# Four-tile products in layers 1 and 2 of a compressed interaction network, and a part boundary at tile 12

## The reference

```
z  = relu(einsum('bhd,bkd,hks->bsd', x0, xk, W) + b)      # layers 0, 1, 2
xk = z[:, :64],  direct += z[:, 64:]                      # after layers 0 and 1
direct += z                                               # after layer 2
logit = sum over d of direct                              # 64 + 64 + 128 = 256 numbers a row
y = relu(relu([logit, dense] @ W1 + b1) @ W2 + b2) @ W3
```

## Time and profile before

| | us |
|---|---|
| median of 3 runs (lowest, highest) | 666.9 (666.8, 668.03) |
| the profiled execution | 669.69 |
| its span, first to last instruction | 667.9 |
| PE busy | 625.5 (94%) |
| DVE busy | 577.0 (86%), 507 instructions |
| POOL busy | 463.2 (69%) |
| ACT busy | 283.8 (42%) |
| mean granted TensorE clock | 0.995 |

### The profile page before, as it was taken

How to read it: one execution, slowest core, us unless ns; L and a number is a source line. 1 busy time by engine, 2 the same in 40 slices (tenths; PEclk the granted TensorE clock), 3 DMA queues, 4 the chain that set the end, 5 groups by cost and what they waited for, 6 DMA issues and landing times.

```text
span 667.9 us, 7153 instructions
## 1 busy us (share of the span) xinstructions
PE 625.5 (94%) x1916; PEld 358.0 (54%) x1916; DVE 577.0 (86%) x507; ACT 283.8 (42%) x341; POOL 463.2 (69%) x277
## 2 busy tenths in 40 slices
PE   0367999999999999999999999999999999999998
PEld 0124555565555555565655555555656555555553
DVE  4138899999999999999999999999999999999670
ACT  3004443544454444534454444444444544445323
POOL 6507768686887878786977878786878878716340
PEclk9997999999999999999999999999999999999999
DMA  6879586694939486785939495875939395862000
GB/s 226 186 189 222 118 202 133 149 199 93 217 84 227 94 195 139 174 174 117 221 80 216 82 218 114 189 159 135 212 93 216 77 225 105 199 131 67 0 1 0
DMA packets 27902, 98.19 MB, mean 147 GB/s; under 512 B 7473, under 2 KB 16433, under 8 KB 19826
## 3 DMA queue, kind: packets, MB, share of 16 engines
q1 hardware_dynamic: 20137, 90.92, 61.1%
q10 hardware_dynamic: 2633, 5.82, 3.0%
q0 software_dynamic: 5120, 1.32, 1.9%
HBM read 94.20 MB, written 3.84 MB: 147 GB/s over the span
## 4 chain that ended last, share of the span: by engine, by line
PE 85%; DVE 5%; DMA 3%; POOL 3%; issue 2%; ACT 1%; ACTq 0%; DVEq 0%; SPq 0%; POOLq 0%
PE z L527 40%; PE z L538 13%; PE z L533 12%; PE z L535 11%; PE z L518 4%; DVE products L405 4%; DMA x_rep<-x_rows 2%; PE z L521 2%; POOL gathered L361 1%; POOL low L309 1%; PE z L520 1%; PE spare L571 1%; PE z L595 1%; DVE low L309 1%; PE xk L595 1%
## 5 line engine op out<-in xcount | busy, mean ns | idle before, releaser
L405 DVE TENSOR_TENSOR products<-x_rep,xk 128x1024 f32<-128x1024 f32 (+1 forms) x288 | 366.7, 1333 | 28.1 <-ACT xk L621 27.2
L309 POOL TENSOR_TENSOR low<-products,high 128x1024 fp32r<-128x1024 f32 x112 | 265.0, 2391 | 134.2 <-ACT high L637 92.9
L527 PE MATMUL z<-products,w_whole 128*128 128x512 f32 x672 | 313.4, 599 | 0.0
L637 ACT ACTIVATE high<-products 128x1024 fp32r<-128x1024 f32 x176 | 184.3, 1056 | 243.0 <-DVE products L405 200.6
L361 POOL DMA_INDIRECT gathered<-in_tables,rows_sb x160 | 197.5, 1235 | 46.5 <-issue 44.2
L533 PE MATMUL z<-high,w_high 128*128 128x512 f32 x352 | 188.2, 535 | 16.5 <-ACT high L637 16.5
L527 PEld LDWEIGHTS z<-products,w_whole 128*128 128x128 f32 x672 | 128.6, 191 | 113.1 <-issue 98.3
L535 PE MATMUL z<-high,w_low 128*128 128x512 f32 x352 | 139.6, 397 | 0.0
L538 PE MATMUL z<-low,w_high 128*128 128x512 f32 x352 | 114.0, 405 | 4.3 <-DVE low L309 3.6
L533 PEld LDWEIGHTS z<-high,w_high 128*128 128x128 f32 x352 | 66.9, 190 | 62.3 <-issue 33.2
L309 DVE TENSOR_TENSOR low<-products,high 128x1024 fp32r<-128x1024 f32 x64 | 93.8, 1467 | 1.3 <-ACT high L637 1.3
(11 more groups left out here) (34 smaller groups left out, 102.8 us busy)
## 6 DMA issues: line engine op xcount, KB each, us to landing
x_rep<-x_rows SPq DMA_DIRECT2D x60, 768.0 KB, 16.4
x_rep<-x_rows SPq DMA_DIRECT2D x61, 512.0 KB, 9.3
x_rows<-gathered SPq DMA_DIRECT2D x15, 225.0 KB
x_rep<-in_w ACTq DMA_DIRECT2D x2, 1280.0 KB, 9.4
gathered<-in_tables,rows_sb POOLq DMA_INDIRECT x160
x_rep<-x_rows SPq DMA_DIRECT2D x4, 384.0 KB, 12.6
x_rep<-x_rows ACTq DMA_DIRECT2D x4, 384.0 KB, 19.0
x_same<-x_rows SPq DMA_DIRECT2D x15, 90.0 KB
```

The source lines that it names most:

```text
L309: ops.tensor_tensor(low[0:p, slot, 0:n, :], products[0:p, index % RING, 0:n, :], high[0:p, slot, 0:n, :].bitcast(fp32), ALU.subtract).then ...
L405: nc.vector.tensor_tensor(slots, rep, row.unsqueeze(1).broadcast_to([p, n, N]), ALU.mult).then_inc(made, 1 + pair)
L527: mm = nc.tensor.matmul(out, w_whole[0:p, at, i, :], products[0:p, slot, i, :], start=(t + i == 0), stop=(t + i == tiles[layer] - 1))
L637: nc.scalar.activation(high[0:p, slot, 0:n, :], products[0:p, index % RING, 0:n, :], ACT.Copy).then_inc(rounded, 1)
```

## The change

DVE makes four tiles in one instruction for eight pairs of groups rather than two: 0+1, 2+3, 4+5 and 6+7 in layer 1, and 14+15, 16+17, 18+19 and 20+21 in layer 2. Groups 6+7 hold tiles 12 to 15, and 20+21 likewise, so a part of the replicated inputs may no longer begin at tile 14: the third part ends at tile 12, and the fourth has eight tiles.

```diff
-PARTS = [(0, 4), (4, 8), (8, 14), (14, T1)]
+PARTS = [(0, 4), (4, 8), (8, 12), (12, T1)]
 FIRST_PARTS = [(0, 2), (2, 4), (4, T0), (T0, 10), (10, 14), (14, 17), (17, T1)]
...
-PAIRED = [0,2]
+PAIRED = [0, 2, 4, 6, 14, 16, 18, 20]
```

## The result

The changed kernel takes 677.99 us (median of 4 executions, 676.19 to 679.49), the kernel before 667.24 us beside it. The ratio is 1.0161, with an interval of 1.0137 to 1.0186: 10.8 us slower. The forecast was 672.2 us, slower by 5.3, with a range of 666.5 to 675.5 us: the direction is right, the size is half of what was measured, and the time lies above the range.

What follows compares the result with a forecast made beforehand. The prediction took a loop of dependences through PE's small stalls for POOL's low parts as the bound. It added 15 turns x 0.35 = 5.3 us, other terms at 0, to 666.9 us: 672.2 us, range 666.5 to 675.5.

Steps and rivals of the forecast that it cites:

- The loop: In each turn PE waits for POOL's low 0; a delay of POOL's low 19 and 21 reaches it one for one.
- The held relu: In layer 2 ACT's relu into direct01 waits for the later sum, holding high 19: 0.35 us a turn, 5.3 us.
- Price of a pair: On DVE one pair comes every 2.19 us by starts, so a pair saves 0.07 us.
- Slots: On DVE pairs wait earlier for a second slot of the ring: cost 0.
- Layer 1, parts: Pairs 4+5 and 6+7 in layer 1, covered by POOL's four low parts, and the changed input parts: cost 0.
- The tail: In the last turn no relu waits for the sum; PE has its own work up to layer 2; the tail stays.
- The base: The median before, 666.9 us, 2.8 us under the profiled execution; the 5.3 us were added to it.
- A: Rival: ACT takes high 19 once pair 18+19 is made; 0.38 us a turn faster, 661.2 us; chance 0.08.
- B: Rival: DVE's stack of group 23 does not wait for POOL; 0.29 us a turn earlier, 662.5 us; chance 0.05.
- C: Rival: no difference; DVE makes a pair every 2.12 us, delay 0.14 us a turn, 669.0 us; chance 0.07.
- D: Rival: DVE's pairs cost their full duration, 2.28 us; 0.62 us a turn slower, 676.2 us; chance 0.10.

Runs made afterwards that it cites:

- e9: e6 with the sum logits01 two groups later on DVE, behind pair 20+21, and ACT's relu into direct01 behind high 21; 661.03 us, ratio 0.9887.
- e1: The changed kernel with the sum logits01 one step earlier on DVE, ahead of the pair 18+19; 667.03 us, ratio 0.9999.
- e2: The changed kernel with ACT's relu into direct01 and its wait moved behind the high part of 19; 667.11 us, ratio 0.9993.
- e3: The kernel before with 18+19 as the only added pair; 675.79 us, ratio 1.0132.
- e5: The changed kernel with DVE's waits for the slots of groups 14 and 15 ahead of its wait for xk1_ready; 674.54 us, ratio 1.0086.
- e7: The kernel before with 14+15 as the only added pair; 670.97 us, ratio 1.0044.
- e11: The changed kernel with the pairs of layer 1 alone and the new parts; 667.78 us, ratio 0.9992.
- e6: The changed kernel with the edits of both e2 (relu behind high 19) and e5 (slot waits ahead of xk1_ready); 661.57 us, ratio 0.9913.

## Why the prediction was right in its sign and wrong in its size

*The loop.* Right. That a delay of POOL's low 19 and 21 reaches PE's first stall through the stack of group 23 was taken from two turns; in the changed kernel the stack takes 1.91 us (1.9 predicted), and in e9, asking 0.4 us before POOL is done, 0.92 us. In all 16 turns of all 14 traces it ends 0.54 to 0.56 us behind POOL's low part, whatever its own duration, 0.75 to 1.92 us.

*The held relu.* Right, and the main cause: e1, e2 and e3 show it from three sides. Step by step, from the start T of layer 2: the sum at T + 7.74 (7.70 predicted), high 19 at T + 9.04 (8.99), low 19 at T + 10.23 (10.19), product 0+1 at T + 15.51 (15.49). So 0.37 us a turn for 0.35. PE's first stall is 0.90 us, not "about 0.7": this 0.37 and the 0.16 us of the slots below, on the 0.35 us that stood there.

*Price of a pair.* One pair every 2.20 us for 2.19. The reading by starts held. The Trainium skill ("VectorE: DVE Perf Modes", section on SBUF-source operations paying a fixed extra latency per instruction) states a fixed term of about 151 cycles for an instruction; an estimate from that figure is 0.157 us for a merge, and that is not what a merge gives back here, 0.07 us. By durations a merge saves 0.14 us, near that term; the starts, not the durations, set the time here.

*Slots.* Here the step failed, a term of the sum put at nothing: "Pairs wait for a second slot of the ring earlier ... Cost 0." I had asked only whether the slot was free, and it was. The wait itself takes instructions, and for 14+15 they stand between `xk1_ready` and the product, on the loop: 0.16 us a turn, 14 x 0.16 = 2.2 us, shown by e5 (taken away, 37.66 to 37.51) and e7 (alone, +0.15). With it the sum is 5.3 + 2.2 + 15 x 0.02 = 7.8 us, against 7.6 in the turns of the profile.

*Layer 1, parts.* Right (e11).

*The tail.* "The tail stays": wrong by 1.7 us in the profiled execution, by the lower clock. This is the second term that was put at nothing, and its cause stays open. The sum 7.6 + 1.7 = 9.3 us lies in both intervals of the comparison (9.1 to 12.4 us and 7.8 to 11.2 us); of the medians, 10.8 and 9.7 us, it leaves 1.5 and 0.4 us that no run explains.

*The base.* The profiled execution of before was 2.4 us above the median now, and I had carried only the difference over; the start of the span moves by up to 4.9 us between executions (47.9 to 52.8), with no bearing on the verdict.

*The rivals.* A, the saved time reaching PE, is false for this order and near the truth once the order is mended: against the kernel before, the turn gains 0.16 us in e2 with the relu out of the way and 0.32 us in e6 with the slot waits moved too, where A had 0.38. B is out by the stack of 1.91 us. C and D named prices of the pair that it does not have. D's 676.2 us is the nearest of all to the 677.99 measured, by luck: pairs come every 2.20 us and not every 2.28.

## What to carry to other kernels

When a merge makes two results with one instruction, look at what stood between them on that engine, here a sum of 0.7 us, and at who in another engine's queue waits for that thing ahead of the results; the first is delayed by the whole second half of the merge (1.1 us in e3, where the sum starts at T + 7.86 instead of T + 6.79). Count waits as instructions: behind the semaphore that arrives last, a further wait that needs instructions of its own can cost time even if it has long been fulfilled (0.16 us here), and belongs ahead of it. Where DVE was not waiting for anything else the pairs' waits cost nothing that shows: e11 adds two pairs in layer 1 and its turn moves by 0.02 us. A change that loses on such an order may be a good one with the order mended: the six pairs cost some 10 us as they stood and were worth 5 to 6 us with two edits.

## What the runs showed of the hardware that was not expected

- In DVE's loop the fulfilled waits for a pair's slots, two short instructions more between the arriving semaphore and the work, take 0.16 us (0.29 against 0.13 us from ACT's end to DVE's start, 0.29 us in e7 too). With them ahead of the arriving semaphore it is 0.13 us (e5).
- The stack of group 23, a DVE instruction of 0.69 us where POOL makes no low part, takes 0.75 to 1.92 us beside one and ends 0.54 to 0.56 us behind it, in every turn of every trace.
- TensorE fell to 1.2 GHz for some 3.5 us in the tail (mean granted clock 0.54 from 665 to 668.5 us in the changed kernel), behind waits of 0.60 us for DVE's sum and 0.22 us for ACT's relus, in six traces and not in eight others with the same code there. It cost 1.7 us there. What decides it is not shown.
- Kernels that are equal up to there start layer 1 at 47.9 to 52.8 us after the first instruction. In those two traces DVE's first product of layer 0 waited 12.5 and 18.8 us for the first transfer of replicated inputs to land. Differences under 0.2% need several executions.
